# Reordering the last steps of every odd head in a four-engine attention pipeline

## The reference

```python
q = jnp.einsum('btm,mhd->bthd', x, w_aq)
k = jnp.einsum('btm,mhd->bthd', x, w_ak)
v = jnp.einsum('btm,mhd->bthd', x, w_av)
q = _rope(q)
k = _rope(k)
s = jnp.einsum('bihd,bjhd->bhij', q, k) / D_HEAD
s = s - INF_APPROX * mask          # mask: i < j
p = jax.nn.softmax(s, axis=-1)
o = jnp.einsum('bhij,bjhd->bihd', p, v)
r = jnp.einsum('bihd,hdm->bim', o, w_ao)
```

## Time and profile before

| | us |
|---|---|
| median of 3 runs | 1011.26 |
| lowest, highest | 1010.4, 1012.74 |
| the profiled execution's own time | 1012.19 |
| its span, first to last instruction | 1010.4 |

### The profile page before, as it was taken

The page is one execution under the profiler, slowest core; times in us unless marked ns, Lnnn a source line. Parts: engine busy times, 40 slices in busy tenths (PEclk is TensorE's granted clock), DMA queues, the critical chain, the costliest instruction groups (busy, mean ns, idle before and its releaser), DMA issues.

```text
span 1010.4 us, 19473 instructions
## 1 busy us (share of the span) xinstructions
PE 969.2 (96%) x5396; PEld 829.3 (82%) x5396; DVE 815.6 (81%) x1786; ACT 696.4 (69%) x1528; POOL 542.7 (54%) x550
## 2 busy tenths in 40 slices
PE   5999999999999999999999999999989999999996
PEld 3778888888888888888888888888878888888884
DVE  5888888888888888888888888888866677586744
ACT  4878888888778888887888888877864343433522
POOL 3666777778666777866677777767780101000000
PEclk9999999999999999999999999999989999999998
DMA  6424343222232322222226222232300000000000
GB/s 192 126 73 115 77 124 82 62 54 63 65 72 68 77 62 53 64 64 66 71 67 192 53 64 53 64 71 64 105 1 1 1 1 22 0 21 0 1 21 22
DMA packets 34491, 61.95 MB, mean 61 GB/s; under 512 B 5632, under 2 KB 8192, under 8 KB 34048
## 3 DMA queue, kind: packets, MB, share of 16 engines
q1 hardware_dynamic: 33296, 58.10, 22.8%
q10 hardware_dynamic: 1136, 3.15, 0.9%
HBM read 19.80 MB, written 5.24 MB: 25 GB/s over the span
## 4 chain that ended last, share of the span: by engine, by line
PE 58%; ACT 13%; DVE 11%; POOL 9%; issue 7%; DMA 1%; DVEq 0%; ACTq 0%; POOLq 0%; SPq 0%
PE psum L346 29%; PE psum L1081 17%; PE psum L452 6%; ACT probs L580 5%; ACT pT L597 4%; POOL probs L834 4%; PE psum L1054 4%; DVE by_cos L737 3%; POOL swapped L845 2%; POOL qk L851 2%; PE psum L1096 2%; DVE by_sin L733 2%; DVE pT L721 2%; DVE neg_max L705 1%; ACT vals L614 1%
## 5 line engine op out<-in xcount | busy, mean ns | idle before, releaser
L834 POOL TENSOR_SCALAR probs<-probs,inv_sum 128x128 f32<-128x128 f32 (+7 forms) x256 | 191.2, 747 | 204.5 <-DVE inv_sum L711 201.7
L346 PE MATMUL psum<-qk 128*128 128x512 f32 (+3 forms) x1152 | 254.6, 348 | 6.1 <-ACT psum L587 3.4
L580 ACT ACTIVATE probs<-psum,neg_max 128x128 f32<-128x128 f32 (+7 forms) x256 | 190.4, 744 | 85.8 <-DVE neg_max L705 60.4
L346 PE MATMUL psum<-pT,vals 128*128 128x512 f32 (+3 forms) x1152 | 243.5, 352 | 0.6 <-DVE pT L721 0.6
L721 DVE TENSOR_TENSOR pT<-psum,pT 128x512 fp32r<-128x512 f32 (+3 forms) x384 | 201.2, 551 | 43.6 <-ACT pT L597 38.9
L346 PEld LDWEIGHTS psum<-qk 128*128 128x128 f32 x1152 | 195.0, 190 | 36.2 <-issue 8.5
L346 PEld LDWEIGHTS psum<-pT,vals 128*128 128x128 f32 x1152 | 188.9, 190 | 23.5 <-DVE pT L721 1.0
L705 DVE TENSOR_REDUCE neg_max<-psum 128x1 f32<-128x128 f32 (+7 forms) x256 | 190.8, 746 | 2.2 <-PE psum L346 1.6
L452 PE MATMUL psum<-ident,probs 128*128 128x128 f32 x1152 | 176.0, 278 | 14.2 <-POOL probs L834 11.7
L597 ACT ACTIVATE pT<-psum 128x512 fp32r<-128x512 f32 (+3 forms) x384 | 170.8, 479 | 25.9 <-PE psum L452 25.0
L1081 PE MATMUL psum<-hid,w 128*128 128x512 f32 x768 | 176.7, 390 | 0.4 <-DVE value L1392 0.4
(11 more groups left out here) (87 smaller groups left out, 796.8 us busy)
## 6 DMA issues: line engine op xcount, KB each, us to landing
swapped<-by_sin SPq DMA_DIRECT2D x256, 128.0 KB, 2.3
w_stage<-qk_split SPq DMA_DIRECT2D x24, 256.0 KB, 2.7
wv_stage<-v_split SPq DMA_DIRECT2D x12, 256.0 KB, 2.7
ffn_raw<-g SPq DMA_DIRECT2D x2, 1024.0 KB, 7.3
out<-y SPq DMA_DIRECT2D x7, 256.0 KB, 2.0
ffn_raw<-xT SPq DMA_DIRECT2D x3, 512.0 KB, 4.8
w_stage<-rT SPq DMA_DIRECT2D x6, 256.0 KB, 2.9
qk_split<-rT SPq DMA_DIRECT2D x6, 256.0 KB, 2.5
```

Of the source, the lines that this page charges most:

```text
L346: ins = nc.tensor.matmul(out_ap, left[a], right[b], start=first and i == 0, stop=last and i == 2, skip_group_check=onto_mask)
L580: nc.scalar.activation(probs[:, ib % 4, :width], score_row(ib), ACT.Exp, bias=neg_max[:, n:n + 1], accum_out=row_sum[:, n:n + 1]).then_inc ...
L834: nc.gpsimd.tensor_scalar(p, p, inv_sum[:, n:n + 1], 1.0, ALU.mult, ALU.mult).then_inc(probs_ready[0], 1)
```

## The change

Three edits. The first concerns tiles that are made while an odd head runs, that is, those of the next even head; the other two concern the odd head itself:

- The tables get a second row. While an even head runs nothing changes. While an odd head runs, tile 3 is summed in step 6 in place of 5, tiles 2 and 3 are rounded in steps 6 and 7 in place of 5 and 6, and get their low parts in steps 7 and 8 in place of 6 and 7. Step 8 is step 0 of the next even head, and there `roped_low` stands behind the normalization of that head's block 1. `rope_tasks` now tries both rows.
- PE, step 6 of odd heads: `attend(head, 0, range(2, 4))` moves from behind `transpose_probs(head, 6)` to ahead of it.
- DVE, step 5 of odd heads: `negative_max(head, 7)` moves from behind `inverse_sum(head, 6)` to ahead of it.

No operation is added or removed, and no DMA.

```diff
--- before.py
+++ after.py
@@ -47,10 +47,10 @@
 ROPE_TILES = [(0, 0), (1, 0), (0, 1), (1, 1)]
 
 
-QK_STEP = (0, 0, 2, 2)
-SUM_STEP = (2, 2, 4, 5)
-HIGH_STEP = (3, 3, 5, 6)
-LOW_STEP = (3, 4, 6, 7)
+QK_STEP = ((0, 0, 2, 2),) * 2
+SUM_STEP = ((2, 2, 4, 5), (2, 2, 4, 6))
+HIGH_STEP = ((3, 3, 5, 6), (3, 3, 6, 7))
+LOW_STEP = ((3, 4, 6, 7), (3, 4, 7, 8))
 V_STEP = (4, 5, 6, 7)
 PV0_PIECES = ({6: range(0, 2), 7: range(2, 4)}, {5: range(0, 2), 6: range(2, 4)})
 PV1_PIECES = {1: range(0, 2), 2: range(2, 4), 3: range(4, 8)}
@@ -69,7 +69,7 @@
     return width, width if ib < 4 else max(2 * P, width - BANK)
 
 
-NQK, NV = len(QK_STEP), len(V_STEP)
+NQK, NV = len(QK_STEP[0]), len(V_STEP)
 PV_BANK = 7
 FILL_BANKS = ((4, 6, 3, 5, 5, 6, 5, 6, 1, 5, 3, 4), (6, 3, 4, 4, 6, 4, 5, 6, 4, 1, 6, 3))
 QK_BANKS = ((1, 5, 5, 4), (5, 4, 5, 6))
@@ -89,7 +89,7 @@
             for nth in range(FIRST_FILL[s], FIRST_FILL[s] + FILLS_OF[s]):
                 uses["t", off, nth] = [FILL_BANKS[off][nth]]
             for j in range(NQK):
-                if QK_STEP[j] == s:
+                if QK_STEP[off][j] == s:
                     uses["qk", off + 1, j] = [QK_BANKS[off][j]]
             for c in range(NV):
                 if V_STEP[c] == NI * off + s:
@@ -280,9 +280,9 @@
 
         found = []
         for j in range(NQK):
-            later, at = divmod(steps[j], NI)
-            if at == s and exists(step_on(head, 1 - later)):
-                found.append((step_on(head, 1 - later), j))
+            for later in range(2):
+                if steps[(head[1] - later) % 2][j] == s + NI * later and exists(step_on(head, 1 - later)):
+                    found.append((step_on(head, 1 - later), j))
         return found
 
     def v_tasks(head, s):
@@ -518,6 +518,8 @@
                     pe.wait_ge(vo_low, 2)
                 if exists(ahead):
                     scores(ahead, (s + 2) % NI)
+                if s == 6 and head[1] and exists(head):
+                    attend(head, 0, PV0_PIECES[1][s])
                 if exists(head):
                     transpose_probs(head, s)
                 for target, j in rope_tasks(head, s, QK_STEP):
@@ -528,7 +530,7 @@
                         ffn.turn_first_r(pe, c, bank("qk", 2, c))
                 for c in v_tasks(head, s):
                     project_v(head[0], b, c)
-                if s in PV0_PIECES[head[1]] and exists(head):
+                if s in PV0_PIECES[head[1]] and exists(head) and not (s == 6 and head[1]):
                     attend(head, 0, PV0_PIECES[head[1]][s])
                 if s in PV1_PIECES and exists(step_on(head, -1)):
                     attend(step_on(head, -1), 1, PV1_PIECES[s])
@@ -776,11 +778,14 @@
                         first_low(j)
                 if odd_of_batch(head, b) and b == 0 and s in X_STEPS:
                     low_of_x(b + 1, X_STEPS.index(s))
+                max_first = s == 5 and head[1] == 1
+                if max_first and exists(head):
+                    negative_max(head, 7)
                 if exists(step_on(head, (s + 1) // NI)) and s != 1:
                     inverse_sum(step_on(head, (s + 1) // NI), (s + 1) % NI)
                 if s == ADD1_STEP:
                     add_head(step_on(head, -1), 1)
-                if exists(step_on(head, (s + 2) // NI)):
+                if exists(step_on(head, (s + 2) // NI)) and not max_first:
                     negative_max(step_on(head, (s + 2) // NI), (s + 2) % NI)
                 if s == ADD0_STEP and not is_last(step_on(head, -1)):
                     add_head(step_on(head, -1), 0)
```

## The result

The changed kernel takes 1015.17 us in the median (1014.95 to 1015.89, 6 runs), the kernel before 1011.13 beside it (1010.3 to 1012.74, 6 runs). The ratio is 1.0036, with a 95% interval of 1.0027 to 1.0046: **slower by about 0.4%, some 4 us**. The predicted 1012.8 is 2.4 us too low; the measured time lies inside the stated range of 1005.5 to 1016.5, but above the likeliest case's own range, which ended at 1014.5.

What follows compares the result with a forecast made beforehand. PE, busy 96%, was taken as the bound, its named wait being for POOL's probabilities. 12 x 0.05 + 3 x 0.21 = 1.23, plus 0.32 in the last head, gave +1.55 us: median 1012.8, range 1005.5 to 1016.5.

Steps and rivals of the forecast that it cites:

- likeliest case: The forecast as reckoned: +1.55 us, median 1012.8, chance 0.42, own range 1010.8 to 1014.5.
- Maximum 7 first: DVE, odd heads: maximum 7 ahead of reciprocal 6 starts exponential 7 on ACT 0.49 us earlier; normalization 6 starts 0.59 later.
- Rival B: Slower: exponential 7's head start is below 0.4; with 0.25, +4.7 us, time 1016.0; chance 0.22.
- Weighted sum ahead of block 6's transposes: PE, odd heads: six matmuls of some 0.70 us cover the delay of block 6's transposes, which then wait 0.07; cost nothing.
- the cover: The weighted sum run on PE ahead of block 6's transposes; without it PE was to stand for 0.77 us.
- The rotation one step later: Odd heads: block 7's transposes 0.49 us earlier; ACT's extra rounding waits 0.17 for POOL; the next head's block 3 +0.05.
- At the batch's end: Three odd heads followed by code outside the loop: no slack counted, the whole +0.21 us at each.
- what is late next: DVE's low halves, reciprocal 1' and normalization 1' 0.21 us later, block 1' transposes 0.1 in hand; no DVE wait added.
- The last head: Very last odd head, no rotation: only the maximum and reciprocal swap acts, making normalization 7 0.32 us later.
- two rivals: Gap recovered, block 3' not held by its mask (1004.2, half 1007.7, chance 0.26); slower, smaller head start (1016.0, 0.22).
- no change: Outcome within the measurable 2.0 us: chance 0.42, against faster 0.27 and slower 0.31.
- The sentence on the Trainium skill: GpSimd contends with two-SBUF-input VectorE instructions: moved sum 0.76 us more, once, beside x's second low half, first pair's odd head.

## Why the prediction came out as it did

**Maximum 7 first: right.** Exponential 7 starts 2.95 us after block 7's first score matmul (335.42 - 332.47), before 3.46 (334.84 - 331.38 in the earlier trace rows): 0.51 gained, 0.49 predicted. Normalization 6 is 0.47 later (3.17 against 2.70), 0.59 predicted. Rival B needed an advance below 0.4 and didn't happen.

**Weighted sum ahead of block 6's transposes: right in the order, wrong in its worth.** They follow it without a wait, as said. But "without the cover PE would stand for 0.77" priced a wait that only takes the place of two others: it is 0.66, and without the move the kernel is as fast (1.0045 against 1.0036, intervals overlapping).

**The rotation one step later: right.** Block 7's transposes come 0.52 earlier (5.80 against 6.32; 0.49 predicted). The rounding follows mask 2' by 0.58 in place of the 0.43 that the pass took in its place, so it waited 0.15 for the sum (0.17 predicted), and the pass is 0.18 later than before (7.49 against 7.31; 0.20 predicted). Block 3' starts at 9.70 against 9.68, so +0.02 where +0.05 was predicted, after an idle time of 0.57. At the batch's end block 3' comes 2.78 us behind block 2' in place of 2.09, with block 2' earlier by 0.53, so some +0.16 there (0.21 predicted).

**The step that failed is "what is late next".** It went through the transposes of block 1' and score block 4' against GpSimd, and stopped. It said that DVE has no wait added; in fact the low halves of block 7's transposes now wait 0.91 for ScalarE's pass in place of 0.23, and start 0.17 later (8.10 against 7.93). And it did not ask who else must be done ahead of block 5'. That block's scores use two PSUM banks, of which bank 3 last held the transposes of block 2' (`FILL_BANKS`, third entry of the even row), so they wait for VectorE's low half of those. Before, that hand-over had next to no slack. VectorE's operation and the load of block 5', in the stretch of the earlier trace rows:

```profile
346.72 0.55 DVE L721 TENSOR_TENSOR pT<-psum,pT 128x384 fp32r<-128x384 f32 x1
...
347.35 1.21 PEld L346 LDWEIGHTS psum<-qk 128*128 128x128 f32 x6
```

346.72 + 0.55 = 347.27, and the load starts 0.08 later, with no idle time in front only because PE arrived at the same moment. After, 347.99 + 0.55 = 348.54, and the load starts 0.06 later, at 348.60, with 0.30 idle. So 0.02 us was all that VectorE had in hand. It was 0.18 late there (15.52 against 15.34 after block 7's first score matmul), as the pass was: its queue ran on from the low halves of block 7 without a pause to maximum 3', exponential 3' took that lateness over, and reciprocal 3' waited for it. Counted from block 7's scores, block 5' starts at 16.13, before at 15.97: **+0.16 a pair where I had +0.05**. Block 4' waits too, for bank 1, which the projection of tile 0 gives back once VectorE's product with the cosine is done, and I had not seen that either, but it starts only 0.05 later than before (12.02 against 11.97), block 3' 0.02.

**The last head was mis-sized as well.** Loads of block 5, 6 and 7's transposes and the first of the feed-forward part, after:

```profile
736.79 0.81 PEld L452 LDWEIGHTS psum<-ident,probs 128*128 128x128 f32 x6
...
741.18 0.74 PEld L452 LDWEIGHTS psum<-ident,probs 128*128 128x128 f32 x7 [1.62 <-POOL probs L839]
744.17 1.57 PEld L452 LDWEIGHTS psum<-ident,probs 128*128 128x128 f32 x8 [2.25 <-POOL probs L839]
...
754.06 10.74 PEld L1059 LDWEIGHTS psum<-yT,w 128*128 128x128 f32 x48
```

Before, with one more row from the feed-forward part:

```profile
734.38 0.81 PEld L452 LDWEIGHTS psum<-ident,probs 128*128 128x128 f32 x6
...
737.65 0.75 PEld L452 LDWEIGHTS psum<-ident,probs 128*128 128x128 f32 x7 [1.33 <-POOL probs L834]
...
740.85 1.57 PEld L452 LDWEIGHTS psum<-ident,probs 128*128 128x128 f32 x8 [1.71 <-POOL probs L834]
...
750.55 10.76 PEld L1054 LDWEIGHTS psum<-yT,w 128*128 128x128 f32 x48
...
763.49 14.85 PEld L1081 LDWEIGHTS psum<-hid,w 128*128 128x128 f32 x66 [0.82 <-DVE value L1392]
```

Block 5's transposes are 2.41 us later after 15 pairs (0.16 each). The feed-forward part is 3.51 later, so the last head added 1.10, not 0.32. The lateness of block 6's transposes was in my sum: 1.12 (3.27 from block 5's before, 4.39 after), 1.15 reckoned. So was GpSimd's, which gave normalization 7 its 0.32. What was missing is VectorE's queue. There the next reciprocal, 7, stands behind three small operations of the layer norm. The first of them before:

```profile
738.34 0.53 DVE L1273 SCALAR_TENSOR_TENSOR work<-rstd 128x8 f32<-128x8 f32 x1
```

Before, it lost 0.36 us beside GpSimd's product (0.53 for an operation of 0.17). After, with GpSimd's work 1.1 later, two of the three lie beside it, and lose 0.22 and 1.04 (last section). That is 0.90 more, and reciprocal 7 and block 7's transposes are late by that: normalization 7 starts at 743.00, 6.21 us behind block 5's transposes against 5.30, and GpSimd, free at 742.37, had waited 0.63 for the reciprocal. The rest of the 1.10, 0.19, comes behind block 7's transposes. Then 0.81 came back. PE's wait of 0.82 at 763.49, for VectorE's `value`, is gone in the changed kernel; that its later start gave VectorE the time is my reading, and no run tests it. I had not looked for such slack behind.

**The sum again**, in spans: 15 x 0.16 = 2.41 (1.23 predicted), 1.10 (0.32), -0.81 (0): 2.70 against 1.55. The extra measured time beyond that is in no row. That the time lies inside 1005.5 to 1016.5 says little for the reckoning: the range is 11 us wide, made up from half of two rivals that did not happen, and of the two terms that were too small by 1.96 together, 0.81 was given back by luck.

The prediction's chances leaned to "no change" because +1.55 us sat just under the bound of 2.0; a sum as near to a bound as that should have had more than 0.10 of its 0.42 on the far side.

The sentence on the Trainium skill had the right subject and the wrong place. In the first pair's odd head VectorE's second low half of x took 0.76 us as before, beside the last 0.2 us of the moved sum. I had also misread: GpSimd did not stand free beside that 0.76 before, but was in the last 0.2 us of another product (67.94 to 69.22). Nothing more was lost there, and the loss was in the last head.

## What to carry to other kernels

A wait that is named over and over in a profile is not worth its length: closing it here won 0.5 us and gave it back within two blocks, because the engine that was to be relieved (PE) takes its next permission from the queue (ScalarE's) into which the work was moved. When work is shifted by a step, walk down the queue that it enters until the first hand-over with slack of its own, through PSUM banks and buffers too, and not only through data; the load that here started 0.08 us behind its releaser, with no idle time shown, had 0.02 in hand. And try the one neighbour more: the same change is +4 us with the rounding ahead of the mask and -5 with it behind.

## What the hardware showed that I had not expected

In the last head GpSimd's product with two operands in SBUF, and VectorE beside it:

```profile
741.10 1.27 POOL L1214 TENSOR_TENSOR w<-ffn_raw,w 128x512 fp32r<-128x512 f32 x1
...
741.18 1.21 DVE L1280 TENSOR_TENSOR work<-work,var 128x8 f32<-128x8 f32 x1
```

VectorE's product of two 128x8 tiles in SBUF began 0.08 us after GpSimd's operation and ended at 742.39, 0.02 after it (742.37): 1.21 us for an operation that takes 0.17 elsewhere. This isn't slowed work but blocked work, for as long as the other engine's instruction lasts. The operation ahead of it (740.75, 0.39 us) ended 0.01 behind GpSimd's normalization 6, and the one of before (738.34, 0.53 us) 0.02 behind GpSimd's product. The same holds for 128x512: the two low halves of x in the earlier trace rows, 0.69 us each where nothing lies beside them (7.1 and 7.7 us into the trace), both ended 0.55 behind GpSimd's product (64.02 behind 63.47, 69.77 behind 69.22). In all of them what is left to do when GpSimd ends is the operation's own time less some 0.14 to 0.16. The Trainium skill (SBUF — State Buffer, "SBUF: two separate sides") says that GpSimd and VectorE share one pair of SBUF ports, which is given to one of them for a whole instruction while the other "fully blocks", where VectorE's instruction has two SBUF inputs; the trace agrees, with 1.21 us for an instruction of 0.17. A tiny VectorE operation with two SBUF inputs can thus cost a full GpSimd instruction, and a reordering, as here, changes which one meets it.
